# Sampling: VectorE adds the halves of an output product behind pairs 11 and 19 of the next quad, in place of 13 and 21

## The chip, the cores and the metric

The kernel runs on one core of a Trainium2 chip. What counts is the device time of one execution in microseconds (us). Smaller is better.

## What is computed

Two layers, each an attention over a context and a feed-forward part, with a residual and a layer norm in front of each of the four parts. The change lies in the third, the deformable sampling attention of the second layer. Cut to it:

```python
# x, ctx: 32 sequences x 128 tokens x 256; H = 16 heads of 16, P = 4 points; inside, B, L = 32, 128
q = layernorm(x)
v = (ctx @ w_value + b_value).reshape(B, L, H, 16).transpose(0, 2, 1, 3)
off = (q @ w_off + b_off).reshape(B, L, H, P, 2)
attw = softmax((q @ w_attw + b_attw).reshape(B, L, H, P), axis=-1)
ix = ((clip(off[..., 0], 0, 1) + 1) * L - 1) * 0.5      # where in the context a point lies
x0 = floor(ix); fx = ix - x0
sampled = v[x0] * ((1 - fx) * m0 * hy) + v[x0 + 1] * (fx * m1 * hy)   # linear between two rows
x = x + einsum('bhlpd,bhlp->blhd', sampled, attw).reshape(B, L, D) @ w_out + b_out
x = x + ffn(layernorm(x))                               # needs the layer norm and the extremes of x
```

## The kernel before

**Sampling as matmuls.** A point that lies between two rows is written as a matrix of weights over the context rows (a "hat" over each position). The 32 sequences are 8 quads of four. A quad takes 16 steps, called pairs (TURN = 16), so there are 128 pairs, n = 0 to 127. For each pair TensorE makes the two sides of the hats in PSUM (`sides`, L1296: two matmuls of 512 columns). Of an even pair ScalarE takes the positive part into `hat` (`relu`, L901). Of the odd pair behind it VectorE takes the positive part and adds the even pair's result (L1746, called the hat of pair n here). GpSimd adds the tiles of two such couples (`sum_points`, L673), and TensorE multiplies that sum with the values into bank 4 (`take`, L1311, 16 small records, behind the pairs 9, 13, 17 and so on). Half a quad's heads done, ScalarE copies bank 4 to `attT` (L907, behind the relus of pairs 6 and 14 of a quad), and TensorE starts bank 4 anew (`clear_att`, L1337, at pairs 0 and 8).

**The output product.** For each quad q, `project_att` multiplies attT with w_out into bank 5, for two of the four sequences at a time (half i = 0, 1), in two steps c = 0, 1. Step c = 0 begins with the bias row (L1323) and has two matmuls (L1326); step c = 1 has two more. TensorE does these while it works on the next quads: behind the pairs 7, 11, 15 and 19 counted from the start of the next quad (`project_slots`; 19 is pair 3 of the quad after). Step c = 0 of a half writes over bank 5, so it waits for the semaphore x3_done, that is until the half before was added to x.

**The add.** VectorE does that: `add_out` (L1760) waits for the product (out_mm, counted at the end of step c = 1) and adds bank 5 to `x_sb`. It stands in VectorE's list behind the hat of pair `add_slots(q)[i]`, counted like the others. One hat later follow the two bn_stats of that half (`two_moments`, L1456), two and three hats later its maximum and minimum (`two_ends`, L1770). Behind each hat there is thus one small piece of such work. Quads 6 and 7 have lists of their own.

**What sets the order.** Each engine runs its list in the order in which it is written and waits at semaphores; there is no scheduler. TensorE may make the sides of pair n when the tile of pair n − 3 has been read (three PSUM tiles take turns): for an even n by VectorE's hat, for an odd n by ScalarE's relu.

Of the kernel before, what the change touches and what calls it, by code (L numbers as in the profile page):

```python
# [36 lines left out]
NQ = B // QUAD  # L37
# [156 lines left out]
def build(nc, x, ctx_in, wq, wk, wv, wo, bq, bk, bv, bo, wfr, wfi, bf, wval, bval, woff, boff,  # L194
# [6 lines left out]
    with ExitStack() as ctx:  # L201
# [266 lines left out]

        def add_slots(q):

            return (13, 21) if q < NQ - 2 else (9, 13)

        def group_at(t, tick):

# [977 lines left out]
        def _(dve):  # L1452
# [289 lines left out]
            def sample_dve(k):  # L1742
                n = 2 * k + 1
                dve.wait_ge(side_mm, n + 1)
                dve.wait_ge(relu_done, k + 1)
                V.scalar_tensor_tensor(ramp(n), sides_of(n)[:].rearrange("p i t -> p (i t)"), 0.0, ramp(n), ALU.max, ALU.add).then_inc(hat_done, 1)  # L1746
                for q in (n // TURN - 1, n // TURN - 2):
                    for i in range(2):
                        t = n - (q + 1) * TURN - add_slots(q)[i]
                        if q >= 0 and t == 0:  # L1750
                            add_out(q, i)
                        if q >= 0 and t == 2:
                            two_moments(q, i)
                        if q >= 0 and t in (4, 6) and n < PAIRS:
                            two_ends(q, i, t // 2 - 2)
# [216 lines left out]
```

## Time and profile before

| | |
|---|---|
| median of three runs | 933.95 us (932.26 to 934.11) |
| profiled execution | 933.78 us |
| its span, first to last instruction | 931.9 us |
| busy over the span | PE (TensorE) 84%, DVE (VectorE) 68%, ACT (ScalarE) 49%, POOL (GpSimd) 28% |
| the chain that ended last | PE 60%, DVE 16%, ACT 14%, issue 6%, DMA 2% |

The profile is of one execution. Its rows name engine, line, operation and tiles (out<-in). PE rows are matmuls, PEld rows weight loads. The sampling loop stands between 418 and some 583 us of the span. "Granted clock" is the share of TensorE's full clock that the chip gave it: 1.00 is 2.4 GHz, 0.50 is 1.2 GHz. The share of busy time over the whole span mixes stages with different limits, so the rows below are of the loop alone.

### The profile page before, as it was taken

How to read it: one execution, taken by the hardware profiler on the slowest of the kernel's cores; microseconds unless marked ns; L12 is line 12 of the kernel's file. 1: busy time of each engine (PE TensorE's matmuls, PEld its weight loads, DVE VectorE, ACT ScalarE, POOL GpSimd, SP SyncE). 2: the span in 40 equal slices, each digit the busy share in tenths (PEclk: the TensorE clock that was granted, in tenths of full speed). 3: DMA queues.
4: the chain of work that ended last, by engine and by line, in shares of the span. 5: the costliest groups of instructions: out<-in, count | busy, mean ns of one | idle time of the engine just before them, and what ended most of it. 6: DMA issues, size and time to landing. Idle time of an engine off the chain costs nothing.

```text
span 931.9 us, 10923 instructions
## 1 busy us (share of the span) xinstructions
PE 783.3 (84%) x3735; PEld 499.4 (54%) x3737; DVE 636.6 (68%) x1176; ACT 456.9 (49%) x801; POOL 256.7 (28%) x200
## 2 busy tenths in 40 slices
PE   3999989789999988878888888899997995009998
PEld 3777766567767666643434435344443442007887
DVE  2466677886687847666776777577747997994333
ACT  2444434454533357655544442233429995963332
POOL 3000000356787302145655453100002330000000
PEclk9999999899999999988998999799999998559999
DMA  8900000013042000000000000000002347810111
GB/s 284 307 1 1 1 0 2 0 58 68 5 135 69 11 2 1 1 1 1 1 1 1 1 1 1 0 1 0 1 0 113 154 162 265 322 66 23 57 46 56
DMA packets 30411, 51.70 MB, mean 55 GB/s; under 512 B 3027, under 2 KB 25619, under 8 KB 29206
## 3 DMA queue, kind: packets, MB, share of 16 engines
q1 hardware_dynamic: 28752, 49.50, 15.5%
q10 hardware_dynamic: 1606, 1.52, 0.5%
q8 instruction: 30, 0.49, 0.2%
q14 instruction: 23, 0.19, 0.1%
HBM read 34.23 MB, written 16.78 MB: 55 GB/s over the span
## 4 chain that ended last, share of the span: by engine, by line
PE 60%; DVE 16%; ACT 14%; issue 6%; DMA 2%; POOL 1%; ACTq 1%; DVEq 0%; SPq 0%; POOLq 0%
PE pair L1394 9%; PE pair L1441 9%; PE pair L1059 5%; PE pair L1167 4%; DVE hat L1746 3%; PE pair L1063 3%; PE pair L1326 3%; DVE wide L1895 2%; PE pair L1337 2%; PE pair L1311 2%; PE pair L1104 2%; PE pair L1296 2%; PE pair L1201 2%; ACT upq L991 2%; ACT g2q L997 2%
## 5 line engine op out<-in xcount | busy, mean ns | idle before, releaser
L1746 DVE SCALAR_TENSOR_TENSOR hat<-pair,hat 128x1024 f32<-128x1024 f32 x64 | 77.7, 1219 | 47.4 <-PE pair L1296 33.2
L901 ACT ACTIVATE hat<-pair 128x1024 f32<-128x1024 f32 x64 | 65.2, 1023 | 81.1 <-PE pair L1296 81.0
L1419 PE MATMUL pair<-xqs,wuT 128*128 128x512 f32 x192 | 84.7, 602 | 4.8 <-ACT up_stage L947 4.8
L673 POOL TENSOR_TENSOR hat<-hat 128x1024 f32<-128x1024 f32 x30 | 70.6, 2352 | 61.6 <-DVE hat L1746 61.6
L1394 PE MATMUL pair<-xqs,wgT 128*128 128x512 f32 x192 | 85.8, 605 | 0.0
L1441 PE MATMUL pair<-wdT,hid 128*128 128x256 f32 x384 | 83.1, 379 | 0.4 <-DVE hid L1943 0.4
L1441 PEld LDWEIGHTS pair<-wdT,hid 128*128 128x128 f32 x384 | 72.9, 190 | 11.1 <-DVE hid L1943 1.2
L565 POOL TENSOR_TENSOR rstd<-lnt,half 128x8 f32<-128x8 f32 (+2 forms) x15 | 26.6, 1776 | 145.9 <-DVE lnt L1485 145.9
L1059 PE MATMUL pair<-wT,ft_sb 128*128 128x256 f32 x256 | 64.8, 397 | 0.0
L1419 PEld LDWEIGHTS pair<-xqs,wuT 128*128 128x128 f32 x192 | 36.9, 194 | 51.3 <-issue 51.1
L1012 ACT ACTIVATE hid<-wide,unit 128x768 f32<-128x768 f32 x32 | 32.6, 1026 | 57.2 <-DVE hid L1943 43.7
L1394 PEld LDWEIGHTS pair<-xqs,wgT 128*128 128x128 f32 x192 | 36.9, 195 | 44.0 <-issue 44.0
L1558 DVE TENSOR_TENSOR ab<-qq,pair 128x512 f32<-128x512 f32 x32 | 22.0, 687 | 54.3 <-ACT qq L743 54.3
L928 ACT ACTIVATE wide<-pair 128x512 f32<-128x512 f32 x48 | 28.7, 597 | 57.4 <-PE pair L1394 57.4
L1496 DVE TENSOR_SCALAR xn<-x_sb,rstd,nmr 128x256 f32<-128x256 f32 x96 | 53.1, 554 | 2.6 <-PE pair L1184 2.3
L1059 PEld LDWEIGHTS pair<-wT,ft_sb 128*128 128x128 f32 x256 | 46.7, 192 | 12.9 <-issue 7.7
L741 ACT ACTIVATE qq<-pair 128x256 f32<-128x256 f32 x32 | 12.3, 383 | 83.0 <-PE pair L1063 83.0
L1943 DVE TENSOR_SCALAR hid<-hid 128x768 f32<-128x768 f32 x32 | 17.9, 560 | 51.1 <-PE pair L1441 49.6
L1434 PE MATMUL pair<-wdT 128*128 128x512 f32 x12 | 8.0, 820 | 52.8 <-DVE peak L1929 52.8
L692 POOL CAST xqs<-xqT 128x1024 f32<-128x1024 int16 x16 | 19.0, 1186 | 116.8 <-ACT xqT L921 78.1
L1456 DVE BATCH_NORM_STATS2 stats<-x_sb 128x6 f32<-128x256 f32 x128 | 50.9, 415 | 0.1
L1296 PE MATMUL pair<-rows,sel 64*128 64x512 bf16 x256 | 43.9, 400 | 4.9 <-DVE hat L1746 2.9
(225 smaller groups left out, 1749.9 us busy)
## 6 DMA issues: line engine op xcount, KB each, us to landing
up_far<-up_stage SPq DMA_DIRECT2D x24, 512.0 KB, 2.6
ups<-up_far SPq DMA_DIRECT2D x8, 1536.0 KB, 7.0
x_sb<-in_x_dram SPq DMA_DIRECT2D x8, 512.0 KB, 7.6
c_sb<-in_ctx_dram SPq DMA_DIRECT2D x8, 512.0 KB, 8.1
ctx<-in_ctx_dram SPq DMA_DIRECT2D x32, 128.0 KB
out_dram<-x_sb SPq DMA_DIRECT2D x16, 256.0 KB, 2.1
ctx<-in_ctx_dram SPq DMA_DIRECT2D x16, 126.0 KB
four<-in_c_four_dram SPq DMA_DIRECT2D x1, 1280.0 KB, 8.5
```

The lines of the kernel that those rows point to most:

```text
L673: nc.gpsimd.tensor_tensor(ramp(4 * u + 2), ramp(4 * u), ramp(4 * u + 2), ALU.add).then_inc(summed, 1)
L901: nc.scalar.activation(ramp(n), sides_of(n)[:].rearrange("p i t -> p (i t)"), ACT.Relu).then_inc(relu_done, 1)
L1012: nc.scalar.activation(hid[:, 2 + s], wide[:, :, at_seq(b)], ACT.Identity, scale=unit[:, 4, 3:4], bias=unit[:, 7, 0:1]).then_inc(o_round, 1)
L1059: mm(bank[2 + s][:, i * D:(i + 1) * D], ft_sb[:, s, i * DC + c, :], wT[:, i, c, :], start=False, stop=(i == 1 and c == DC - 1))
L1167: last = mm(bank[6 + s][:, 0:D], tr_sb[:, s, c, :], fold[:, c, :], start=False, stop=(c == DC - 1))
L1296: last = mm(sides_of(n)[:, i, :], sel[half, n % NP, :], rows[half, q, c * 2 + a, :], start=True, stop=True)
L1394: last = mm(bank[2 + oc][:], wgT[:, c, oc * 128:(oc + 1) * 128], xqs[:, s, c, :], start=(c == 0), stop=(c == DC - 1))
L1419: last = mm(bank[2 + oc], wuT[:, c, oc * 128:(oc + 1) * 128], xqs[:, t % 2, c, :], start=(c == 0), stop=(c == DC - 1))
L1441: last = mm(bank[s][:, 0:D], hid[:, s, ic, :], wdT[:, ic, :], start=(ic == 0), stop=(ic == IC - 1))
L1456: V.bn_stats(stats[:, at(b), :].rearrange("p o s -> p (o s)"), x_sb[:, at(b), :].rearrange("p o d -> p (o d)")).then_inc(bn_done[n], 1)
L1496: V.tensor_scalar(xn[:, b % 4, :], x_sb[:, at(b), :].rearrange("p o d -> p (o d)"), rstd[:, at(b)], nmr[:, at(b)], ALU.mult, ALU.add).then ...
L1746: V.scalar_tensor_tensor(ramp(n), sides_of(n)[:].rearrange("p i t -> p (i t)"), 0.0, ramp(n), ALU.max, ALU.add).then_inc(hat_done, 1)
```

## The change

The places of the adds for the quads 0 to 5 go from 13 and 21 to 11 and 19. All that VectorE does for a half behind the add is counted from the same number, and moves with it.

```diff
         def add_slots(q):
 
-            return (13, 21) if q < NQ - 2 else (9, 13)
+            return (11, 19) if q < NQ - 2 else (9, 13)
```

VectorE's list at the first half of quad 0, of the kernel before (hat is that of pair 25 in the first row, and of pairs 27, 29, 31, 33 and 35 in the next; pair2 is bank 5's half of the PSUM tiles):

```order
L1746 SCALAR_TENSOR_TENSOR hat<-pair1,hat 128x1024
L1746 SCALAR_TENSOR_TENSOR hat<-pair0,hat 128x1024
L1746 SCALAR_TENSOR_TENSOR hat<-pair3,hat 128x1024
L1760 TENSOR_TENSOR x_sb<-pair2,x_sb 128x512
L1746 SCALAR_TENSOR_TENSOR hat<-pair1,hat 128x1024
L1456 BN_STATS stats<-x_sb 128x6 x2
L1746 SCALAR_TENSOR_TENSOR hat<-pair0,hat 128x1024
L1770 TENSOR_REDUCE ends<-x_sb 128x2
L1746 SCALAR_TENSOR_TENSOR hat<-pair3,hat 128x1024
L1770 TENSOR_REDUCE ends<-x_sb 128x2
```

The same place on VectorE in the changed kernel:

```order
L1746 SCALAR_TENSOR_TENSOR hat<-pair1,hat 128x1024
L1746 SCALAR_TENSOR_TENSOR hat<-pair0,hat 128x1024
L1760 TENSOR_TENSOR x_sb<-pair2,x_sb 128x512
L1746 SCALAR_TENSOR_TENSOR hat<-pair3,hat 128x1024
L1456 BN_STATS stats<-x_sb 128x6 x2
L1746 SCALAR_TENSOR_TENSOR hat<-pair1,hat 128x1024
L1770 TENSOR_REDUCE ends<-x_sb 128x2
L1746 SCALAR_TENSOR_TENSOR hat<-pair0,hat 128x1024
L1770 TENSOR_REDUCE ends<-x_sb 128x2
L1746 SCALAR_TENSOR_TENSOR hat<-pair3,hat 128x1024
```

The add (L1760) and the three pieces behind it each stand one hat earlier. The same holds for all twelve halves of quads 0 to 5; the lists of TensorE, ScalarE, GpSimd and SyncE are the same in both kernels.

At the end of the loop VectorE's list of the kernel before reads, from the hat of pair 117 on:

```order
L1746 SCALAR_TENSOR_TENSOR hat<-pair0,hat 128x1024
L1760 TENSOR_TENSOR x_sb<-pair2,x_sb 128x512
L1746 SCALAR_TENSOR_TENSOR hat<-pair3,hat 128x1024
L1456 BN_STATS stats<-x_sb 128x6 x2
L1746 SCALAR_TENSOR_TENSOR hat<-pair1,hat 128x1024
L1760 TENSOR_TENSOR x_sb<-pair2,x_sb 128x512
L1770 TENSOR_REDUCE ends<-x_sb 128x2
L1746 SCALAR_TENSOR_TENSOR hat<-pair0,hat 128x1024
L1456 BN_STATS stats<-x_sb 128x6 x2
L1770 TENSOR_REDUCE ends<-x_sb 128x2
```

and in the changed kernel, from the hat of pair 115 on:

```order
L1746 SCALAR_TENSOR_TENSOR hat<-pair1,hat 128x1024
L1760 TENSOR_TENSOR x_sb<-pair2,x_sb 128x512
L1746 SCALAR_TENSOR_TENSOR hat<-pair0,hat 128x1024
L1456 BN_STATS stats<-x_sb 128x6 x2
L1746 SCALAR_TENSOR_TENSOR hat<-pair3,hat 128x1024
L1770 TENSOR_REDUCE ends<-x_sb 128x2
L1746 SCALAR_TENSOR_TENSOR hat<-pair1,hat 128x1024
L1760 TENSOR_TENSOR x_sb<-pair2,x_sb 128x512
L1770 TENSOR_REDUCE ends<-x_sb 128x2
L1746 SCALAR_TENSOR_TENSOR hat<-pair0,hat 128x1024
L1456 BN_STATS stats<-x_sb 128x6 x2
L1746 SCALAR_TENSOR_TENSOR hat<-pair3,hat 128x1024
```

Quad 6's own first add, the second L1760 here, stays behind the hat of pair 121; the work of quad 5 has moved one hat up against it, so that one of its reduces shares the hat of pair 121 as before and none is left behind that of pair 123.

## Rows read from the trace of the kernel before

**Rows 1.** Stretches: busy us (records) of PE, PEld, DVE, ACT, POOL, granted clock, DMA
```profile
447.00:559.00 112.00, 94.20 (x651) 44.77 (x652) 80.38 (x102) 51.55 (x57) 61.46 (x33) 0.92 0.00 1
600.00:705.00 105.00, 97.29 (x260) 44.52 (x258) 67.45 (x66) 41.54 (x76) 8.32 (x8) 1.00 0.00 0
```
**Rows 2.** Waits, 447 to 559: who <- for whom: us in total, times, longest
```profile
PE pair L1323 <- DVE x_sb L1760: 16.6, 11, 1.5
```
**Rows 3.** Timeline of PE, bias matmuls: start, us, what, [idle before <- releaser]
```profile
448.20 0.37 PE L1323 MATMUL pair<-bias,small 3*128 3x512 bf16 x1 [1.39 <-ACT attT L907]
...
487.04 0.37 PE L1323 MATMUL pair<-bias,small 3*128 3x512 bf16 x1 [1.51 <-DVE x_sb L1760]
...
547.63 0.37 PE L1323 MATMUL pair<-bias,small 3*128 3x512 bf16 x1 [1.51 <-DVE x_sb L1760]
558.49 0.37 PE L1323 MATMUL pair<-bias,small 3*128 3x512 bf16 x1 [1.51 <-DVE x_sb L1760]
```
**Rows 4.** The chain that ended last, at the same place: start, us, what
```profile
466.08 0.61 DVE x_sb L1760
466.69 0.14 issue
```
**Rows 5.** Timeline of PE over one half quad (pairs 43 to 55)
```profile
462.11 1.13 PE L1326 MATMUL pair<-wout_sb,attT 128*128 128x256 f32 x4
...
464.71 0.60 PE L1296 MATMUL pair<-rows,sel 64*128 64x512 bf16 x4
466.82 0.37 PE L1323 MATMUL pair<-bias,small 3*128 3x512 bf16 x1 [1.51 <-DVE x_sb L1760]
...
468.19 0.39 PE L1296 MATMUL pair<-rows,sel 64*128 64x512 bf16 x2
468.50 1.12 PE L1337 MATMUL pair<-w63m,v63m 128*128 128x512 f32 x2
469.56 0.39 PE L1296 MATMUL pair<-rows,sel 64*128 64x512 bf16 x2
...
470.88 0.61 PE L1296 MATMUL pair<-rows,sel 64*128 64x512 bf16 x4
471.42 1.13 PE L1326 MATMUL pair<-wout_sb,attT 128*128 128x256 f32 x4
...
473.02 1.07 PE L1311 MATMUL pair<-hat,v_sb 128*32 128x128 f32 x16
...
476.13 0.37 PE L1323 MATMUL pair<-bias,small 3*128 3x512 bf16 x1 [1.51 <-DVE x_sb L1760]
```
**Rows 6.** Timeline of DVE over the same half quad
```profile
463.13 1.22 DVE L1746 SCALAR_TENSOR_TENSOR hat<-pair,hat 128x1024 f32<-128x1024 f32 x1 [0.63 <-ACT hat L901]
464.27 0.68 DVE L1770 TENSOR_REDUCE ends<-x_sb 128x2 f32<-128x512 f32 x1
464.86 1.21 DVE L1746 SCALAR_TENSOR_TENSOR hat<-pair,hat 128x1024 f32<-128x1024 f32 x1
466.00 0.68 DVE L1760 TENSOR_TENSOR x_sb<-pair,x_sb 128x512 f32<-128x512 f32 x1
...
467.72 0.74 DVE L1456 BATCH_NORM_STATS2 stats<-x_sb 128x6 f32<-128x256 f32 x2
470.00 1.22 DVE L1746 SCALAR_TENSOR_TENSOR hat<-pair,hat 128x1024 f32<-128x1024 f32 x1 [1.53 <-PE pair L1296]
...
472.44 1.22 DVE L1746 SCALAR_TENSOR_TENSOR hat<-pair,hat 128x1024 f32<-128x1024 f32 x1 [0.63 <-ACT hat L901]
```
**Rows 7.** Timeline of ACT at the same place
```profile
466.06 0.59 ACT L907 ACTIVATE attT<-pair 128x512 f32<-128x512 f32 x1
```
**Rows 8.** Timeline of POOL at the same place
```profile
467.88 2.35 POOL L673 TENSOR_TENSOR hat<-hat 128x1024 f32<-128x1024 f32 x1 [1.09 <-DVE hat L1746]
```
**Rows 9.** Stretches, columns as in rows 1: the first and last at half clock
```profile
476.92:480.33 3.41, 3.41 (x7) 0.97 (x6) 0.85 (x3) 1.02 (x1) 3.13 (x3) 0.50 0.03 5
...
548.60:552.01 3.41, 3.41 (x9) 0.79 (x7) 0.67 (x3) 1.02 (x1) 2.35 (x1) 0.50 0.00 0
```

## The prediction

> **What bounds the kernel now.** I read the busy times by stretch first, then the waits, then the chain that ended last, and at the end the engines' timelines side by side over one half of a quad. The change touches only the sampling loop, and of that the part from the second quad on, 447 to 559 us of the span. There TensorE is busy 94.20 of 112 us, VectorE 80.38, ScalarE 51.55 and GpSimd 61.46, and TensorE's granted clock is 0.92 on average [rows 1]. So TensorE is idle for 17.8 us, and the list of waits tells where: the first matmul of an output product (the bias row, L1323) waits eleven times for x_sb, the add on L1760, 16.6 us together [rows 2], and a twelfth time for 1.39 us, put down to attT [rows 3]; there the add ended just before, so I count it with the others. 16.6 + 1.39 = 18.0 us: within the accuracy of the rows this is all the idle time that TensorE has in the stretch. The chain shows the same place from the other side: it leaves VectorE through the add, 0.14 us of handing over, and goes on at the bias matmul [rows 4].
>
> One half quad in detail. The pairs have numbers from 0; pair 47 has place 15 in its quad. TensorE issues pairs 46 and 47 from 464.71 [rows 5]. By the rows of pairs 50 and 51 (470.88, next matmul 471.42 [rows 5]) two pairs occupy it 0.54 us, so it is ready for the output product of the second half at 465.25. It starts at 466.82 with 1.51 us of idle time in front [rows 5]. What it waits for is on VectorE: the hat of pair 43 at 463.13, a reduce of an earlier half at 464.27 (0.68 us), the hat of pair 45 at 464.86, and only then the add, 466.00 to 466.68 [rows 6]. From one bias matmul to the next it is 9.31 us (466.82 to 476.13), of which 1.51 is this stall [rows 5]: TensorE's own work for half a quad takes 7.80 us.
>
> **The change, part by part.** No instruction is added or removed. In every half of quads 0 to 5 the add stands one hat earlier, and the bn_stats pair and the two reduces of that half follow it one hat earlier too. VectorE issues no DMA here and no queue but its own changes.
>
> *The add comes earlier.* In the half above, the add of 0.68 us takes the place that the reduce has now, behind the hat of pair 43: 464.27 to 464.95 [rows 6]. With 0.14 us of handing over [rows 4] the bias matmul may go at 465.09. TensorE gets there at 465.25. So the wait goes whole, with 0.16 us in hand. Its price today is 1.39 + 16.6 = 18.0 us in twelve places.
>
> *Does the add now wait itself?* It needs the second matmuls of the output product before, which TensorE issues behind pair 43: 462.11 to 463.24 [rows 5]. The add would start at 464.27, 1.03 us later. It does not wait, so nothing queued behind it (the hat of pair 45 first of all) is held up. I take zero; the upper end is in the rivals.
>
> *What is late next?* I shift TensorE and see which wait it meets. Product at 465.25, taking 1.37 us (466.82 to 468.19 [rows 5]), so pair 48 at 466.62. Pair 48 needs the hat of pair 45, which ends at 466.07 as now [rows 6], plus 0.14: 466.21, early by 0.41. The clearing matmul behind it, at 466.93 (0.31 us later, as 468.19 to 468.50 [rows 5]), needs the copy of attT, 466.06 plus 0.59 plus 0.14: 466.79, early by 0.14 [rows 7]. The clearing takes 1.06, pair 49 follows at 467.99. The hat of pair 49 starts 0.44 us behind it as today (469.56 to 470.00 [rows 5, 6]), at 468.43; VectorE is free for it at 464.86 + 1.14 (hat and on to the next, as 464.86 to 466.00) + 0.74 (bn_stats, in the place of the add) + 1.14 + 0.59 (reduce) = 468.47 [rows 6]. So that hat moves from 470.00 to 468.47 and everything behind it by about the same 1.5 us. Pairs 50 and 51 start at 469.31 on TensorE, 1.57 us earlier than the row at 470.88 [rows 5]; the hat of pair 51, which waits for ScalarE's relu of pair 50, starts 1.56 us behind that row today (472.44 [rows 6]) and so at 470.87. TensorE reaches the next output product at 472.99 (476.13 less the old stall with its 0.06 us of rounding, 1.57, and less the 1.57 gained before), and the add behind pair 51 is done with the same 0.16 us in hand. The pattern repeats at 7.7 to 7.8 us for half a quad. GpSimd's sum is not in the way: it ends at 470.23 [rows 8], the matmuls that take it start at 473.02 [rows 5], and moved to 471.45 they still stand 1.0 us or more behind a sum that also moves with its hat. So TensorE becomes the bound of the loop with hardly any idle time, and VectorE needs some 7.0 us of its 7.8.
>
> *The clock.* Five times in this stretch TensorE runs at half of the full clock, 1.2 in place of 2.4 GHz, for 3.41 us; the first and the last of the five have their rows [rows 9]. The first half quad with such a fall takes 10.91 us from bias matmul to bias matmul (476.13 to 487.04), the last 10.86 (547.63 to 558.49 [rows 3, 5]), against 9.31: 1.60 and 1.55 us more, some 7.9 us for five. The first fall begins 0.79 us after the end of a stall of 1.51 us, the last 0.97 us after another; the other three stand likewise, and none comes without a stall in front. Where TensorE works on with little idle time, as from 600 to 705 us (97.29 of 105 us busy), the clock stays at 1.00 [rows 1]. I take it that with the stalls the falls go too: 7.9 us, with zero as the other end. The page "TensorE: Matmul & The Clock Gate" of the Trainium skill speaks both ways here. Its section "HAM oscillation — how this bites in real kernels" puts the falling clock down to waits longer than any in these rows; by it the five falls have another cause and the sum is 915.8. Its section "A second HAM failure mode: psum-queue depth-cycling" tells of short idle times between groups of matmuls that make the clock swing; by it the sum is 907.9. The rows, with their falls right behind stalls of 1.51 us, are nearer to the second.
>
> *The end of the loop.* Quads 6 and 7 keep their places. The reduces of quad 5 come one hat earlier, so one of them no longer shares a hat with the bn_stats of quad 6. I count nothing for it.
>
> **The sum.** The profiled execution took 933.78 us (span 931.9). 933.78 − 18.0 − 7.9 = 907.9. The median of the runs lies 0.17 us above the profiled one, so 908.0 for the median.
>
> **Rivals.** (1) The stalls go and the clock still falls. 933.8 − 18.0 = 915.8. For it: the falls may belong to something in the mix of matmuls. Against it: each of the five has a stall in front. 13%.
>
> (2) The stall is replaced by a shorter one. The loop that goes over pair 50, its relu, the hat of pair 51, the add and back to the bias matmul has only 0.16 us in hand, and the attT copy 0.14. If two handings-over come 0.2 us later each when engines work closer together, some 0.3 us of wait is left in each half: 12 times 0.3 is 3.6, so 911.5. Should half of every stall come back and the falls stay away, 917. 10%.
>
> (3) Nothing comes of it, 933: the wait moves to another instruction of TensorE in the same place, the hat of pair 45 before pair 48. It has 0.41 us in hand by the walk above and would have to be 1.9 us late. That the add is not where the change says belongs here as well; the order of the instructions shows it there. 4%.
>
> (4) Slower: VectorE stands at the add. The second matmuls of the product would have to end over 1.03 − 0.14 = 0.89 us later than now, measured against the hat; then the hat of pair 45 waits with it, then TensorE's pair 48 and the output product. It decides against the change when this wait passes 0.89 + 0.16 + 1.51 = 2.56 us of lateness, since only then more is lost than the old stall; with 3.1 us the time would be 933.8 + 12 × 0.54 = 940. Nothing in the rows makes these matmuls so late: they follow pair 43 directly on TensorE, and pair 43 is what the hat needs. 4%.
>
> **How the numbers follow.** The forecast, stalls and falls gone, has 69%; its own range is 904 to 911.5, since the walk gives 7.7 rather than 7.8 us for half a quad (12 × 0.1 below) and the falls elsewhere in the span may come out differently by a few us. The range of 8 in 10 reaches up over rivals (1) and (2): 904 to 917. A measurement of this kernel can tell about 0.2%, 1.9 us, from no change. Faster by more than that: 69 + 13 + 10 = 92%. Within it: 4%. Slower: 4%.
>
> **What the profile after will show.** If the steps are right, the bias matmul on L1323 has no wait for x_sb in quads 1 to 5, bias matmuls follow at 7.7 to 7.8 us, TensorE's idle time between 447 us and the end of the loop falls below 2 us, the rows of the granted clock show 1.00 there, and the loop ends some 26 us earlier while all later stages take what they take now. Rival (1) shows as no wait but stretches at 0.50; rival (2) as waits below 0.8 us before L1323 or L1337; rival (4) as idle time of VectorE before L1760, released by L1326. The forecast is wrong if the distance of bias matmuls stays above 8.3 us.

## The result, and the profile after

| | median of its runs | ratio to the kernel before, same chip | 95% interval |
|---|---|---|---|
| before | 933.75 us (932.26 to 934.11, 4 runs) | 1 | |
| after | 906.82 us (906.53 to 908.18, 4 runs) | 0.9716 | 0.9692 to 0.974 |

26.9 us less, where 908.0 was forecast in a range of 904 to 917. The profiled execution of the changed kernel took 906.77 us with a span of 905.0, so the two profiled ones differ by 27.0 us.

The stretches of the changed kernel, in the columns of [rows 1]: the first is the loop as long as the moved adds have to do with it, the second its end, where quads 6 and 7 have their own places.

```profile
447.00:537.00 90.00, 90.00 (x680) 45.33 (x679) 82.29 (x105) 52.68 (x58) 63.95 (x34) 1.00 0.01 1
537.00:549.00 12.00, 9.92 (x107) 6.12 (x105) 9.92 (x21) 3.80 (x5) 0.77 (x2) 1.00 0.01 1
```

TensorE is busy for 90.00 of 90 us, where it had 94.20 of 112 [rows 1], and its clock is 1.00, where it had 0.92. The loop up to 537 us now holds TensorE's own work and no idle time. The list of waits over 417 to 559 us answers [rows 2]:

```profile
PE pair L1323 <- DVE x_sb L1760: 1.6, 2, 0.9
```

The two that are left belong to quads 6 and 7. One half quad on TensorE, against [rows 5]:

```profile
454.07 0.60 PE L1296 MATMUL pair<-rows,sel 64*128 64x512 bf16 x4
454.60 0.38 PE L1323 MATMUL pair<-bias,small 3*128 3x512 bf16 x1
...
455.98 0.39 PE L1296 MATMUL pair<-rows,sel 64*128 64x512 bf16 x2
456.30 1.12 PE L1337 MATMUL pair<-w63m,v63m 128*128 128x512 f32 x2
...
458.68 0.60 PE L1296 MATMUL pair<-rows,sel 64*128 64x512 bf16 x4
459.21 1.13 PE L1326 MATMUL pair<-wout_sb,attT 128*128 128x256 f32 x4
...
462.35 0.38 PE L1323 MATMUL pair<-bias,small 3*128 3x512 bf16 x1
```

The bias matmul stands 0.53 us behind the pairs in front of it, with no idle time in brackets, and the next one 7.75 us later (454.60 to 462.35; 9.31 before). VectorE over the same piece, against [rows 6]:

```profile
452.49 1.22 DVE L1746 SCALAR_TENSOR_TENSOR hat<-pair,hat 128x1024 f32<-128x1024 f32 x1 [0.63 <-ACT hat L901]
453.63 0.68 DVE L1760 TENSOR_TENSOR x_sb<-pair,x_sb 128x512 f32<-128x512 f32 x1
454.23 1.21 DVE L1746 SCALAR_TENSOR_TENSOR hat<-pair,hat 128x1024 f32<-128x1024 f32 x1
455.36 0.74 DVE L1456 BATCH_NORM_STATS2 stats<-x_sb 128x6 f32<-128x256 f32 x2
456.02 1.21 DVE L1746 SCALAR_TENSOR_TENSOR hat<-pair,hat 128x1024 f32<-128x1024 f32 x1
...
457.79 1.23 DVE L1746 SCALAR_TENSOR_TENSOR hat<-pair,hat 128x1024 f32<-128x1024 f32 x1
...
460.24 1.22 DVE L1746 SCALAR_TENSOR_TENSOR hat<-pair,hat 128x1024 f32<-128x1024 f32 x1 [0.63 <-ACT hat L901]
```

The add ends at 454.31, 0.29 us before the bias matmul starts, of which 0.14 are the handing over: 0.15 us in hand. It does not wait for its product (no bracket in front of L1760). VectorE's wait of 1.53 us in front of a hat is gone; 0.63 us for ScalarE is left in each half.

### The profile page after: what moved, and what is told of

Read it like the earlier page. It is cut to its first block, busy times and chain, and to the rows that moved or that the text cites. A ratio compares the mean times of both kernels' runs of the same rounds, so it can differ in the third digit from the quotient of the medians.

```text
span 905.0 us, 10925 instructions
## 1 busy us (share of the span) xinstructions
PE 774.4 (86%) x3737; PEld 497.3 (55%) x3737; DVE 635.7 (70%) x1176; ACT 456.8 (50%) x801; POOL 257.1 (28%) x200
## 4 chain that ended last, share of the span: by engine, by line
PE 65%; ACT 13%; DVE 12%; issue 6%; DMA 2%; POOL 1%; ACTq 1%; DVEq 0%; SPq 0%; POOLq 0%
PE pair L1394 9%; PE pair L1441 9%; PE pair L1059 5%; PE pair L1296 4%; PE pair L1326 4%; PE pair L1311 4%; PE pair L1167 4%; PE pair L1063 3%; DVE wide L1895 3%; PE pair L1104 2%; PE pair L1337 2%; PE pair L1201 2%; ACT upq L991 2%; ACT g2q L997 2%; PE pair L1041 2%
## 5 line engine op out<-in xcount | busy, mean ns | idle before, releaser
L1296 PE MATMUL pair<-rows,sel 64*128 64x512 bf16 x256 | 42.6, 390 | 5.0 <-DVE hat L1746 2.9
```

What stands on the lines that cost most here:

```text
L1296: last = mm(sides_of(n)[:, i, :], sel[half, n % NP, :], rows[half, q, c * 2 + a, :], start=True, stop=True)
```

## The experiments

Two questions were open behind the number. First, whether the two terms (waits 18.0, falls of the clock 7.9) are the right split, and whether the falls come from the stalls at all. Second, how narrow the place is: how much is in hand, and what an add costs that stands too early or too late.

| kernel | median | before, same chip | ratio | interval |
|---|---|---|---|---|
| stalls filled with matmuls | 925.39 | 932.33 | 0.9915 | 0.9897 to 0.9933 |
| only the first half's add moved (11, 21) | 916.13 | 932.33 | 0.981 | 0.9785 to 0.9836 |
| adds one hat earlier than after (9, 17) | 912.86 | 932.33 | 0.9786 | 0.9765 to 0.9807 |
| the add alone moved | 908.25 | 932.33 | 0.9738 | 0.9716 to 0.9761 |
| adds one hat later than before (15, 23) | 978.84, one run | 936.28 | 1.045 | |
| after, once more | 906.0 | 936.28 | 0.9689 | 0.9665 to 0.9712 |
| after, TensorE kept at work behind the loop | 905.46 | 936.28 | 0.9675 | 0.9651 to 0.9699 |

**Stalls filled, waits kept.** The kernel before, with work put into TensorE's idle time:

```diff
-                for i in range(2):
+                for i in (0, 1) * (6 if n % 8 == 7 and 31 <= n <= 119 else 1):
                     half = slice(i * 64, (i + 1) * 64)
                     last = mm(sides_of(n)[:, i, :], sel[half, n % NP, :], rows[half, q, c * 2 + a, :], start=True, stop=True)
                 last.then_inc(side_mm, 1)
```

> The kernel before, with its adds at 13 and 21. In the twelve places where TensorE stood for 1.4 to 1.5 us in front of a bias matmul, it makes the sides of the pair in front of it (places 7 and 15) six times instead of once, into the same place, and signals after the last: 5 x 0.27 = 1.35 us more of work in the time of the stall. The add and the bias matmul stay where they are. Theory (the stalls of TensorE bring the clock down): the waits for x_sb are still paid in time, but with little idle time left in them the five falls of the clock go; 933.8 - 7.9 = 925.9 us, granted clock 1.00 in the loop. Rival (the falls belong to the mix of matmuls, and went in the changed kernel for another reason): the five falls stay, 933.8 us, or more if the repeated sides run at half clock.

Its TensorE timeline at one such place, and the stretch of [rows 1] there:

```profile
473.51 1.69 PE L1296 MATMUL pair<-rows,sel 64*128 64x512 bf16 x14
475.62 0.37 PE L1323 MATMUL pair<-bias,small 3*128 3x512 bf16 x1 [0.43 <-DVE x_sb L1760]
```

```profile
447.00:559.00 112.00, 106.27 (x809) 52.63 (x807) 84.53 (x107) 53.09 (x59) 63.37 (x34) 1.00 0.00 1
```

The first and the last of the twelve bias matmuls, against the first and last of [rows 3]:

```profile
447.69 0.37 PE L1323 MATMUL pair<-bias,small 3*128 3x512 bf16 x1 [0.30 <-ACT attT L907]
...
550.11 0.37 PE L1323 MATMUL pair<-bias,small 3*128 3x512 bf16 x1 [0.43 <-DVE x_sb L1760]
```

The ten more matmuls stand in front of the bias matmul, the wait behind them has shrunk to 0.43 us, and the bias matmuls follow at 9.31 us as before (466.31 to 475.62, the matmul a half earlier). Nothing was gained in the waits. But the clock is 1.00 throughout, and the time fell by 0.85%, 7.9 us of 933.75 (6.3 to 9.6 by the interval). The loop's own rows say the same more finely: from the first to the last of the twelve bias matmuls it is 102.42 us, where it was 110.29 [rows 3], 7.87 less. So the second term of the sum stands by itself and has its size: the idle time in the stalls made the clock fall, and it cost 7.9 us. The mix of matmuls alone did not: in the changed kernel it is the same as before, and no fall comes.

**Half of the change.** Against the kernel before:

```diff
-            return (13, 21) if q < NQ - 2 else (9, 13)
+            return (11, 21) if q < NQ - 2 else (9, 13)
```

> Half of the change: only the first half's add goes from 13 to 11, the second stays at 21. Theory: the waits at place 15 go (six, 1.39 + 5 x 1.51 = 8.9 us), the six at place 7 stay, at about 1.39 us each since the hat in front of that add has no other work before it (0.7 us less together); behind the hat of place 11 now stand two pieces, so the hat of place 13 is 0.59 us later than the 0.41 us in hand and five pairs wait some 0.2 us (1 us more). 933.8 - 8.6 = 925.2 us by the waits alone, and 917 to 925 with the falls of the clock, of which those stay that the six remaining stalls bring. Rival (one late add is enough to keep the old pace, since the half behind it catches up): 931 to 934 us.

Two bias matmuls of its TensorE timeline that stand one behind the other, one that follows a moved add and one that does not, the add in front of the second, its waits over 440 to 562 us, and the stretch:

```profile
464.75 0.38 PE L1323 MATMUL pair<-bias,small 3*128 3x512 bf16 x1
466.24 0.39 PE L1296 MATMUL pair<-rows,sel 64*128 64x512 bf16 x2
...
474.06 0.37 PE L1323 MATMUL pair<-bias,small 3*128 3x512 bf16 x1 [1.38 <-ACT attT L907]
```

```profile
473.24 0.68 DVE L1760 TENSOR_TENSOR x_sb<-pair,x_sb 128x512 f32<-128x512 f32 x1
```

```profile
PE pair L1323 <- ACT attT L907: 8.3, 6, 1.4
```

```profile
447.00:544.00 97.00, 88.47 (x669) 43.75 (x663) 82.15 (x104) 52.16 (x58) 63.34 (x34) 1.00 0.00 1
```

The waits are as expected: gone in every other place, 1.38 us in the others. (The wait is put down to attT; the add is what came last, as in [rows 3]: it ends at 473.92, and 0.14 us later the bias matmul starts.) The pair behind the output product comes 0.11 us late (464.75 to 466.24, where the changed kernel has 454.60 to 455.98), with 0.2 expected. The time is 0.981 of before, 916.0 us on the scale of 933.75 (913.7 to 918.4 by the interval), at the lower end of the 917 to 925: the six stalls that are left bring no fall of the clock at all. So the waits add up place by place, some 925 by themselves, and the falls do not: half of the stalls removed was enough for all 7.9 us. The rival that one late add keeps the old pace is out.

**Too early.** Against the changed kernel:

```diff
-            return (11, 19) if q < NQ - 2 else (9, 13)
+            return (9, 17) if q < NQ - 2 else (9, 13)
```

> The adds one hat earlier still, at 9 and 17, in front of the product that they need (places 11 and 19 on TensorE). Theory: VectorE now stands at the add. In the changed kernel's trace the hat of place 9 starts at 457.79, the second product's matmuls run 459.21 to 460.34; the add can go at 460.48, the next hat at 461.07 in place of 460.24, ends 0.14 us of handing over later than pair 46 needs: TensorE waits about 0.6 us in each half, 12 x 0.62 = 7.5 us, 906.8 + 7.5 = 914.3 us, with idle time of VectorE in front of L1760 put down to L1326, 12 times some 1.4 us. Rival (VectorE has time to spare, its wait costs nothing): 906.8 us. Rival (the standing add holds the whole loop up, as in the slower case of the prediction): over 933.8 us.

Its waits over 440 to 540 us, one place on VectorE, two bias matmuls that stand one behind the other, and the stretch:

```profile
DVE x_sb L1760 <- PE pair L1326: 13.9, 12, 1.4
PE pair L1296 <- DVE hat L1746: 4.6, 12, 0.4
```

```profile
459.66 1.21 DVE L1746 SCALAR_TENSOR_TENSOR hat<-pair,hat 128x1024 f32<-128x1024 f32 x1
462.01 0.69 DVE L1760 TENSOR_TENSOR x_sb<-pair,x_sb 128x512 f32<-128x512 f32 x1 [1.15 <-PE pair L1326]
462.62 1.22 DVE L1746 SCALAR_TENSOR_TENSOR hat<-pair,hat 128x1024 f32<-128x1024 f32 x1
```

```profile
464.43 0.39 PE L1323 MATMUL pair<-bias,small 3*128 3x512 bf16 x1
...
472.63 0.39 PE L1323 MATMUL pair<-bias,small 3*128 3x512 bf16 x1
```

```profile
447.00:537.00 90.00, 85.81 (x652) 42.61 (x649) 77.42 (x100) 50.31 (x55) 60.33 (x32) 1.00 0.00 1
```

VectorE stands at the add for 1.15 us, and the hat behind it stands with it: this is the mechanism of rival (4), in a mild form. TensorE then waits 0.4 us for a hat in each half. A half quad takes 8.20 us in place of 7.75, 5.4 us in twelve. 0.9786 of 933.75 is 913.8 us, 6.5 us more than the changed kernel by the ratios, whose intervals allow 5.4 as well, and still 20 us less than before, since the waits on TensorE are short and the clock stays up. Expected were 914.3, from waits of 0.62 us; they are 0.4, so that the time came out so close is in part luck.

**What is in hand.** The add moved, the bn_stats and the reduces left where they were, against the changed kernel:

```diff
-                        if q >= 0 and t == 2:
+                        if q >= 0 and t == (4 if q < NQ - 2 else 2):
                             two_moments(q, i)
-                        if q >= 0 and t in (4, 6) and n < PAIRS:
-                            two_ends(q, i, t // 2 - 2)
+                        if q >= 0 and t in ((6, 8) if q < NQ - 2 else (4, 6)) and n < PAIRS:
+                            two_ends(q, i, t // 2 - (3 if q < NQ - 2 else 2))
```

> The add alone is moved to 11 and 19; the bn_stats and the reduces stay where they were. So behind places 11 and 3 stand two pieces: at 11 the add and then a reduce, at 3 a reduce and then the add. It measures what the changed kernel has in hand. Theory (0.16 us in hand at the add, 0.41 at the hat of place 13): where the reduce comes first the add is 0.59 us later and TensorE waits 0.43 us for x_sb in front of the bias matmul of place 7; where the add comes first no wait for x_sb, but the next hat is 0.59 us later and the pair behind the output product waits 0.18 us. 6 x (0.43 + 0.18) = 3.7 us over the changed kernel, 910.5 us, clock at 1.00. Rival (what counts is the order of the add alone, there is more in hand): 906.8 us. Rival (nothing in hand): 6 x (0.59 + 0.59) = 7.1, 913.9 us.

VectorE where the reduce comes in front of the add, and the bias matmul that waits for it:

```profile
466.49 1.23 DVE L1746 SCALAR_TENSOR_TENSOR hat<-pair,hat 128x1024 f32<-128x1024 f32 x1 [0.63 <-ACT hat L901]
467.64 0.68 DVE L1770 TENSOR_REDUCE ends<-x_sb 128x2 f32<-128x512 f32 x1
468.23 0.68 DVE L1760 TENSOR_TENSOR x_sb<-pair,x_sb 128x512 f32<-128x512 f32 x1
```

```profile
469.06 0.37 PE L1323 MATMUL pair<-bias,small 3*128 3x512 bf16 x1 [0.38 <-DVE x_sb L1760]
...
476.79 0.38 PE L1323 MATMUL pair<-bias,small 3*128 3x512 bf16 x1
478.28 0.39 PE L1296 MATMUL pair<-rows,sel 64*128 64x512 bf16 x2
...
485.10 0.37 PE L1323 MATMUL pair<-bias,small 3*128 3x512 bf16 x1 [0.38 <-DVE x_sb L1760]
```

The add is 0.59 us later (468.23 in place of 467.64) and costs a wait of 0.38 us, about what 0.16 us in hand leaves of it (0.43). Where the add comes first, the pair behind the output product starts 1.49 us behind the bias matmul (476.79 to 478.28) in place of 1.38, 0.11 us late where 0.18 was expected. From bias matmul to bias matmul one half takes 7.73 and the other 8.31 us: 16.04 for the two against 15.50 in the changed kernel, 0.54 us more, and 3.2 in the loop, with 0.61 and 3.7 expected. The ratio, 0.9738 against 0.9716, says 2 us, with intervals that overlap; the loop's own rows are the finer measure here. The place in the list matters to a few tenths of a us: a single reduce in front of the add is felt.

**Too late.** Against the kernel before:

```diff
-            return (13, 21) if q < NQ - 2 else (9, 13)
+            return (15, 23) if q < NQ - 2 else (9, 13)
```

> The other direction: the adds one hat later than in the kernel before, at 15 and 23. Theory: the bias matmul then waits for the hat of place 15 and the add behind it. In the rows of before that hat starts at 466.59, so the add would run 467.72 to 468.40 and the bias matmul start at 468.54 in place of 466.82: 1.72 us more in each of twelve places, 20.6 us, 954 us with the same five falls of the clock and up to 965 if each of the longer stalls brings one. Rival (the place only decides whether there is a stall, not how long): 934 us.

Its waits over 447 to 602 us, a bias matmul, and the second of the stretches at half clock with the one behind it, then the last:

```profile
PE pair L1323 <- DVE x_sb L1760: 38.5, 12, 3.2
```

```profile
491.74 0.58 PE L1323 MATMUL pair<-bias,small 3*128 3x512 bf16 x1 [3.23 <-DVE x_sb L1760]
```

```profile
463.54:470.37 6.83, 6.30 (x19) 2.59 (x21) 0.97 (x2) 1.02 (x1) 3.88 (x3) 0.50 0.01 2
470.37:477.20 6.83, 4.36 (x44) 2.24 (x40) 5.95 (x9) 3.56 (x4) 2.36 (x1) 1.00 0.00 0
...
600.08:606.91 6.83, 5.81 (x12) 2.92 (x13) 0.87 (x2) 1.02 (x1) 2.34 (x1) 0.50 0.00 0
```

The waits are right: 38.5 us where 12 × 3.23 were worked out, 20.5 more than before. The time is not: 978.84 us against 954 to 965. It is one run, but its trace shows the falls one by one: every one of the twelve stalls now brings a fall of the clock, and each lasts 6.83 us, twice as long as the five from 447 us on in the kernel before. What I had wrong is the price of a fall behind a longer stall, not the stall: by the time, 42.6 us more than the kernel before on the same chip, of which 20.5 are waits, the twelve falls cost 30.0 us (42.6 − 20.5 + 7.9), 2.5 each, where 1.6 was counted.

**TensorE kept at work behind the loop.** The lesson on the clock, tried in another place of the changed kernel:

```diff
-            keep_busy(24, bank[3])
+            keep_busy(28, bank[3])
             ...
             spread_peak(0)
+            keep_busy(9, bank[3])
```

> The changed kernel with TensorE kept at work behind the loop, too, by the filling matmuls that the kernel already uses: 28 in place of 24 in front of the spreading of the first peak (some 0.9 us more, in an idle time of 1.0 us) and 9 new ones behind it (some 2.0 us, in an idle time of 2.27 us in front of the turning of the quantised x). Theory (what the stalls taught holds there too: idle time brings the clock down): the stretch of 10.24 us at half clock from 562.2 on goes or gets shorter; the gate matmuls behind it start at 568.9 at half clock, so some 3.5 us of TensorE's work would run twice as fast, 1.7 us, and the turning in front up to 1 us: 904 to 905.5 us where the changed kernel has 906.8. Rival (the fall comes from the waits for VectorE that go on until 568.9 and cannot be filled, or that part is bound by VectorE): 906.8 us. Rival (the filling matmuls come in the way of the peak): up to 1 us slower.

TensorE in front of the turning of x, first in the changed kernel run beside it, then in this one, and the stretch at half clock that follows, again first in the changed kernel:

```profile
560.09 0.44 PE L1383 MATMUL pair<-big,xn 128*128 128x128 f32 x2 [2.27 <-DVE xn L1853]
```

```profile
559.01 2.10 PE L1247 MATMUL pair<-rows,idn 128*128 128x512 bf16 x9
561.45 0.44 PE L1383 MATMUL pair<-big,xn 128*128 128x128 f32 x2 [0.33 <-DVE xn L1853]
```

```profile
561.38:568.21 6.83, 5.93 (x16) 3.21 (x17) 6.12 (x16) 2.58 (x7) 2.32 (x2) 0.50 0.00 0
```

```profile
564.31:571.14 6.83, 5.75 (x13) 2.75 (x12) 5.05 (x11) 1.73 (x5) 1.85 (x2) 0.50 0.00 0
```

The idle time of 2.27 us is filled to 0.33, yet the clock still falls, at 564.3 us. Nor is the fall shorter: the 10.24 us of the expectation are those of the first trace of the changed kernel, and the changed kernel run beside this one has 6.83 us, as this one has. So the length of this fall differs between executions of one kernel. 905.46 us lies where it was expected if the fall went, but the changed kernel beside it took 906.0: 0.9675 against 0.9689 with intervals that overlap, no difference that these runs can tell. The shorter waits that go on behind the filled one were not filled, so whether they bring the fall stays open. No kernel here beats the changed one by more than the measurement can tell.

## Why the prediction was right

*The add comes earlier: right.* All twelve moved waits are gone; the walk through one half quad said 7.7 to 7.8 us, the rows say 7.75.

*The add does not wait: right,* and the run with the adds at 9 and 17 shows from where on it would.

*What is late next: right.* Nothing is late up to 537 us; TensorE's own work sets the pace. The 0.16 us in hand that I worked out at the add are 0.15 in the trace, and the run with the add alone moved felt a delay of 0.59 us as a wait of 0.38.

*The clock: right,* and the part that most needed a run, since it was inferred from falls that stand behind stalls. The run with filled stalls shows 7.9 us for it, by the ratio and by the loop's rows. Of the two sections of the page "TensorE: Matmul & The Clock Gate" of the Trainium skill, "A second HAM failure mode: psum-queue depth-cycling" agrees with the run with filled stalls (falls with idle times of 1.51 us, clock at 1.00 with 0.43 left of them); the other, "HAM oscillation — how this bites in real kernels", would have had the falls stay. The run with half of the change adds what the prediction did not say: the falls go before the last stall has gone.

*The sum: 25.9 against 27.0.* The waits were a little too small. I priced one by its idle time, 1.51 us, and put the 0.06 us between a record's end and the next possible start into the range. By the distance of bias matmuls a half quad lost 9.31 − 7.75 = 1.56 us; eleven of these and 1.45 for the first (9.20 behind the bias matmul in front of it, 439.00 to 448.20, and 7.75 now, 439.11 to 446.86) are 18.6 in place of 18.0. With 7.9 that is 26.5 by the last of the twelve bias matmuls, and the rows agree: from the bias matmul in front of the first to the last it was 119.49 us and is 92.96 now, first before, then after:

```profile
439.00 0.39 PE L1323 MATMUL pair<-bias,small 3*128 3x512 bf16 x1
558.49 0.37 PE L1323 MATMUL pair<-bias,small 3*128 3x512 bf16 x1 [1.51 <-DVE x_sb L1760]
```

```profile
439.11 0.39 PE L1323 MATMUL pair<-bias,small 3*128 3x512 bf16 x1
532.07 0.38 PE L1323 MATMUL pair<-bias,small 3*128 3x512 bf16 x1
```

The other 0.5 us came outside this part, in stages that the change does not touch, and were not forecast.

*One line on the profile after was wrong:* I wrote that TensorE's idle time falls below 2 us up to the end of the loop. It is 0.00 up to 537 us, but 2.08 us from there to 549, and 0.87 more in front of the last bias matmul at 551.83: the waits of quads 6 and 7, which were there before (0.69, 1.39 and 0.88 us), had slipped my count. They cost the sum nothing.

## What to carry to other kernels

Where one engine writes over a buffer that another must first read, look for the reader's place in its own in-order list: if other work stands between the moment its input is ready and the read, moving the read forward can take the whole wait; here it did, and cost nothing, since the input still came first. Walk one period with the durations of the trace, and say how much is in hand at each wait; here it was 0.15 us at the add. Against the changed kernel, one hat earlier cost 5.4 us in the loop; one hat later is the kernel before, 26.9 us; and one hat later still cost another 42.6, in one run. Price a stall of TensorE with what its clock does behind it: here that was 30% of the gain.

## What the hardware showed that I had not expected

The falls of the clock did not go in proportion to the number of stalls. Twelve stalls of about 1.5 us, one every 9.31 us or more, brought five falls of 3.41 us; six of 1.38 us, one about every 17 us, brought none; twelve of 0.43 us, with work in front of them, none; twelve of about 3.2 us brought twelve falls of 6.83 us each. Stalls about twice as long thus cost more than twice as much: 68.5 us (42.6 over the kernel before on one chip, 978.84 against 936.28, and the 25.9 that the stalls and falls cost there). The falls alone cost 30.0 us in place of 7.9. Whether the length of a stall, the distance between stalls or the idle time in all decides was not told apart: these runs change more than one of them at a time. Behind the loop, filling the longest idle time did not keep the clock up; which idle time brings that fall was not found.
